# Alternating the transposes of a step with the score products in an attention kernel's TensorE queue

## The reference

```
h = layernorm(x) * (1 + ca) + sa
q = h @ wq + bq ; k, v = split(h @ wkv + bkv)          # 16 heads in 4 groups, head size 128
q, k = q + pe, k + pe                                  # a table of positions
probs = softmax(where(causal, q @ k.T / sqrt(128), -inf))
x = x + ga * ((probs @ v) @ wo)
h = layernorm(x) * (1 + cb) + sb
x = x + gb * moe(h)                                    # the best 2 of 8 experts, 256 -> 256
```

## Time and profile before

| | us |
|---|---|
| time, median of 3 runs | 930.61 (929.87 to 931.41) |
| span of the profiled execution | 929.5 |
| busy in it: TensorE products / weight loads | 904.2 / 782.2 |
| busy in it: VectorE / ScalarE / GpSimd | 782.4 / 535.9 / 274.5 |
| one steady frame | 22.4 |

### The profile page before, as it was taken

One profiled execution on the slowest core, in us unless ns is written; L12 is line 12 of the kernel. 1 busy time (PEld: TensorE's weight loads), 2 busy tenths in 40 slices (PEclk: granted clock), 3 DMA queues, 4 the chain that ended last, 5 costly groups with the idle time before them and its releaser, 6 DMA issues.

```text
span 929.5 us, 18019 instructions
## 1 busy us (share of the span) xinstructions
PE 904.2 (97%) x5353; PEld 782.2 (84%) x5353; DVE 782.4 (84%) x1775; ACT 535.9 (58%) x1224; POOL 274.5 (30%) x346
## 2 busy tenths in 40 slices
PE   5999999999999999999999999999999999999997
PEld 4788888888888888978888888888888889767775
DVE  6677888888888888888888888888888888899996
ACT  4587666666666666655666666666666655422231
POOL 4454222222222222133322222222222212466544
PEclk9999999999999999999999999999999999999999
DMA  6000000000000000100000000000000022100000
GB/s 215 7 12 13 12 13 12 11 17 17 11 11 11 11 11 7 57 6 1 24 12 12 14 12 11 11 11 11 11 11 11 12 86 81 46 12 18 23 17 24
DMA packets 23764, 21.60 MB, mean 23 GB/s; under 512 B 1530, under 2 KB 22564, under 8 KB 23716
## 3 DMA queue, kind: packets, MB, share of 16 engines
q1 hardware_dynamic: 23652, 20.99, 7.1%
q10 hardware_dynamic: 64, 0.02, 0.0%
HBM read 18.91 MB, written 2.10 MB: 23 GB/s over the span
## 4 chain that ended last, share of the span: by engine, by line
PE 87%; DVE 7%; issue 3%; ACT 2%; POOL 1%; DMA 1%; DVEq 0%; SPq 0%; POOLq 0%; ACTq 0%
PE ps_t L701 13%; PE ps_s L596 10%; PE ps_s L598 10%; PE ps_s L597 9%; PE ps_o L596 7%; PE ps_o L598 7%; PE ps_o L597 6%; PE ps_m L596 6%; PE ps_m L598 6%; PE ps_m L597 6%; PE ps_o L711 1%; PE ps_m L937 1%; PE ps_t L596 1%; PE ps_s L681 1%; DMA wmod_sb<-in_L_wmod_dram 1%
## 5 line engine op out<-in xcount | busy, mean ns | idle before, releaser
L992 ACT ACTIVATE pt_hi<-ps_t 128x512 fp32r<-128x512 f32 (+2 forms) x320 | 170.8, 534 | 143.3 <-PE ps_t L701 143.2
L1042 ACT ACTIVATE probs<-ps_s,neg_max 128x128 f32<-128x128 f32 (+7 forms) x256 | 189.8, 742 | 78.7 <-DVE neg_max L1336 74.4
L1345 DVE TENSOR_TENSOR pt_lo<-ps_t,pt_hi 128x512 fp32r<-128x512 f32 (+2 forms) x320 | 192.5, 602 | 12.6 <-ACT pt_hi L992 7.6
L1336 DVE TENSOR_REDUCE neg_max<-ps_s 128x1 f32<-128x128 f32 (+7 forms) x256 | 192.7, 753 | 3.7
L701 PE MATMUL ps_t<-ident,probs 128*128 128x128 f32 x1152 | 188.7, 272 | 2.1 <-DVE pt_lo L1345 2.1
L483 POOL TENSOR_TENSOR q_lo<-raw,q_hi 128x512 fp32r<-128x512 f32 x60 | 77.4, 1290 | 359.1 <-ACT q_hi L992 359.1
L701 PEld LDWEIGHTS ps_t<-ident,probs 128*128 128x128 f32 x1152 | 141.7, 140 | 27.1 <-DVE pt_lo L1345 8.9
L596 PE MATMUL ps_s<-k_hi,q_lo 128*128 128x512 f32 (+2 forms) x354 | 148.8, 420 | 2.3 <-ACT probs L1042 2.3
L1383 DVE SCALAR_TENSOR_TENSOR acc<-ps_m,rsum,acc 128x256 f32<-128x256 f32 x256 | 111.6, 478 | 24.3 <-PE ps_m L598 24.3
L1330 DVE TENSOR_TENSOR ps_s<-ps_s,mask 128x128 f32<-128x128 f32 x256 | 75.8, 296 | 56.9 <-PE ps_s L598 50.1
L598 PE MATMUL ps_s<-k_hi,q_hi 128*128 128x512 f32 (+2 forms) x354 | 123.5, 349 | 0.0
(11 more groups left out here) (180 smaller groups left out, 1718.0 us busy)
## 6 DMA issues: line engine op xcount, KB each, us to landing
wq_raw<-in_L_attn_wq_dram SPq DMA_DIRECT2D x32, 128.0 KB, 2.2
wo_raw<-in_L_attn_wo_dram SPq DMA_DIRECT2D x32, 128.0 KB, 2.0
wkv_raw<-in_L_attn_wkv_dram SPq DMA_DIRECT2D x2, 1024.0 KB, 6.5
we_raw<-in_L_ffn_expert_w_dram SPq DMA_DIRECT2D x1, 2048.0 KB, 10.1
x_again<-in_L_attn_x_dram SPq DMA_DIRECT2D x2, 1024.0 KB, 9.3
out_dram<-y_out SPq DMA_DIRECT2D x16, 128.0 KB, 1.7
acc<-in_L_attn_x_dram SPq DMA_DIRECT2D x2, 512.0 KB, 3.9
wmod_sb<-in_L_wmod_dram SPq DMA_DIRECT2D x2, 512.0 KB, 8.0
```

Source lines behind the costliest of these rows:

```text
L992: return nc.scalar.activation(dst, src, ACT.Copy, scale=scale)
L1042: nc.scalar.activation(probs[par][:, prob_offset(i):prob_offset(i) + w], ps_s[:, i % 2, col:col + w], ACT.Exp, bias=neg_max[:, par, i:i + ...
L1336: nc.vector.tensor_reduce(neg_max[:, par, i:i + 1], ps_s[:, i % 2, col:col + w], AXIS_X, ALU.max, negate=True).then_inc(max_set, 1)
L1345: nc.vector.tensor_tensor(pt_lo[:, q % PT, lo:CH], ps_t[:, q % 2, lo:CH], pt_hi[:, q % PT, lo:CH].bitcast(F32), ALU.subtract).then_inc(pt_ ...
```

## The change

In a frame that has a next head, all steps but 0 and 10 call a new function, `turn_and_score`, in the place of `turn_probs` and `score_piece`. It has the same waits and issues the same instructions, in another order: first transpose, first score product, second transpose, second product, third transpose, third product, then what is left of the transposes. The wait for the exponential stands in front of the first score product, and so ahead of all transposes but the first. The last transpose still releases ScalarE and the third product VectorE.

```diff
+            def turn_and_score(n, par, q, first, g):
...
+                tiles = list(range(max(j, c * TPC), (c + 1) * TPC))
+                turned = turn(tiles[0])
+                i, c0, w, ends = PIECES[q]
+                if i in (1, TPC) and q == FIRST_PIECE[i]:
+                    pe.wait_ge(q_lo_set, (n + 1) * NC + (i // TPC + 1))
+                if q == FIRST_PIECE[i]:
+                    pe.wait_ge(exp_set, (n + 1) * NT + (i - 1))
...
+                nc.tensor.matmul(out, q_lo[1 - par][:, rows], k_hi[:, g, keys], start=True, stop=False)
+                for t in tiles[1:2]:
+                    turned = turn(t)
+                nc.tensor.matmul(out, q_hi[1 - par][:, rows], k_lo[:, g, keys], start=False, stop=False)
+                for t in tiles[2:3]:
+                    turned = turn(t)
+                scored = nc.tensor.matmul(out, q_hi[1 - par][:, rows], k_hi[:, g, keys], start=False, stop=True)
+                if ends:
+                    scored.then_inc(s_mm, 1)
+                for t in tiles[3:]:
+                    turned = turn(t)
+                turned.then_inc(t_mm, 1)
...
                 for q in range(NS):
-                    turn_probs(n, par, q, first)
+                    mixed_step = nxt and q not in (0, 10)
+                    if mixed_step:
+                        turn_and_score(n, par, q, first, (l + 1) % G)
+                    else:
+                        turn_probs(n, par, q, first)
...
-                    if nxt:
+                    if nxt and not mixed_step:
                         score_piece(n + 1, 1 - par, (l + 1) % G, q, False)
```

More of the change, by code:

```diff
@@ L702, in turn_probs, with turn @@
                 last.then_inc(t_mm, 1)
+            def turn_and_score(n, par, q, first, g):
+                c, j = STEPS[q]
+                if j == 0:
+                    pe.wait_ge(exp_set, n * NT + (c + 1) * TPC)
+                if (q - 2) % NS in LAST_STEP and not (first and q < 2):
+                    pe.wait_ge(pt_hi_set, n * NS + (q - 1))
+                elif not (first and q < 2):
+                    pe.wait_ge(pt_lo_set, n * CUTS + cuts_before(max(q - 1, 0)))
+                def turn(i):
+                    p0 = prob_offset(i) + j * P
+                    col = (i - c * TPC) * P
+                    return pe.transpose(ps_t[:, q % 2, col:col + P], probs[par][:, p0:p0 + P], ident[:, :])
+                tiles = list(range(max(j, c * TPC), (c + 1) * TPC))
[5 more added lines that the diff above has]
+                    pe.wait_ge(exp_set, (n + 1) * NT + (i - 1))
+                rows = slice(i * P, (i + 1) * P)
+                col = score_offset(i) + c0
+                keys = slice(c0, c0 + w)
+                out = ps_s[:, i % 2, col:col + w]
+                nc.tensor.matmul(out, q_lo[1 - par][:, rows], k_hi[:, g, keys], start=True, stop=False)
[10 more added lines that the diff above has]
+                turned.then_inc(t_mm, 1)
             def weigh_values(n, g, q, first):
```

## The result

The changed kernel takes 946.09 us (median of 4 runs, 945.48 to 946.92) against 931.01 us for the kernel before on the same chip; the ratio is 1.0161, 95% interval 1.0147 to 1.0175. The forecast was 947.1. The span of the profiled execution is 943.7 us (929.5 before), and a steady frame takes 22.85 us (22.41; medians of 20 steady frames, from the first transpose's load of one frame to that of the next). 30 x 0.446 = 13.4 us are in the steady pace. The first frames of the two batch halves lost 0.84 and 0.90 us, together 0.9 more than two steady frames, and with these the 14.2 us between the two spans are accounted for within 0.1.

A forecast was written before the change was run, and what follows sets the result against it. TensorE's full queue bounds the kernel. Per frame 0.25 + 0.04 + 0.21 + 0.05 = 0.55 us, times 30 = 16.5 us; span 929.5 becomes 946.0, plus 1.1 gives 947.1 us; range 934 to 954.

The forecast's parts named there:

- The price of a transpose: In TensorE's queue a transpose costs 0.11 us, whether four stand in a row or one stands between products.
- Rival C: Faster: the next product's load hides under the product before; gain 33 us, 898 us; chance 0.05.
- Changeovers: 20 new pairs of switches between transposes and products per frame cost TensorE 0.13 us, bounds 0 and 0.20.
- Steps 2 and 3: Score product stalls 0.10 us for the first exponential; the next step's wait for VectorE swallows half, leaving about 0.05.
- Step 4: Score product waits 0.17 us for row tile 2's exponential, three transposes queued behind it; the step ends 0.25 us later.
- Step 6: Value product waits 0.21 us for the output's low part on VectorE; 0.50 us late, TensorE itself 0.29 late.
- Steps 7 to 9: Only switches cost, 0.05 us; VectorE and ScalarE run up to 1.2 us later but VectorE catches up within the frame.
- rival D: Lateness of ScalarE and VectorE carries into the next frame; about 0.9 us a frame, 957.6 us; chance 0.08.
- A: Only the switches between transposes and products cost: 3.9 us, 934.5 us; chance 0.08.
- B: The score product's wait costs, the value product's wait for the output's low part does not: 10.2 us, 940.8; chance 0.14.
- E: Nothing measurable, as TensorE's queue reaches every wait later than thought: 930.6 us; chance 0.05.
- The sign to look for: TensorE's wait list gains some 30 score-product and some 30 value-product entries, about 0.2 us each; frames 22.95 us.

The follow-up runs named there:

- the kernel with two transposes ahead: Changed kernel with step 5 in the old order and two transposes ahead of the score product at step 4: 936.13 us, ratio 1.0060.
- the new step 0: Kernel before, with step 0's first score product ahead of the six query products: 929.16 us, ratio 0.9983; timed again 929.41 us, 0.9981.
- the output first: Changed kernel, but at step 5 ScalarE and VectorE take the output's high and low parts before the transposed block's: 940.40 us, ratio 1.0104.

## Why the prediction was right, point by point

- **What bounds.** Right: what held the queue in a frame came back in the time at least thirty times over. The whole change and the three kernels with one wait or only steps 4 and 5 alternated gave 3.4 to 3.6 us for each 0.1 us; the kernel with two transposes ahead gave more, 5.4 us for 0.12.
- **The price of a transpose.** Right that the order doesn't change it: 0.11 us in a row and 0.11 alternated. Rival C (a faster kernel) is excluded by the frames of 22.44 and 22.32 us with six steps alternated, and by the spacing that it named: in the changed step 6, with a transpose between them, the loads of the 512-wide products are 0.34 and 0.35 us apart, where C wanted under 0.30.

```profile
298.66 0.19 PEld L730 LDWEIGHTS ps_s<-k_hi,q_lo 128*128 128x128 f32 x1
...
299.00 0.19 PEld L733 LDWEIGHTS ps_s<-k_lo,q_hi 128*128 128x128 f32 x1
...
299.35 0.19 PEld L736 LDWEIGHTS ps_s<-k_hi,q_hi 128*128 128x128 f32 x1
```

- **Changeovers.** The term that was mis-sized. I took 0.13 us a frame for 20 pairs; 14 pairs cost at most 0.03 us in the frame (22.44 against 22.41) and 0.1% (0.02 to 0.20%) in the time, and with the new step 0 nothing (22.32 with and without). The 0.01 us by which a transpose follows a 256-wide product late isn't lost at each changeover. This is most of the 0.10 us a frame by which the forecast was too high (3 us); the first frames of the two halves, which I took for ordinary ones, gave 0.9 back. So the span was forecast at 946.0 and is 943.7, 2.3 us less. That the time came within 1.0 us is in part luck: the 1.1 us that I took from span to time is 1.8 within one execution, and the median before moved up by 0.4 us with its fourth run.
- **Steps 2 and 3.** The stall at step 2 was 0.10 as forecast; step 3 swallowed all of it, not half. The first transpose of step 4 starts 7.07 us into the frame in both kernels (290.40 - 283.33, 295.35 - 288.28). The weight loads' list of waits shows the idle time that took it up, first before and then after. It also corrects my reading of TensorE's list, in which this wait seemed to be 2.1 us in the whole run:

```profile
PEld ps_t L701 <- DVE pt_lo L1345: 8.9, 33, 1.0
```

```profile
PEld ps_t L701 <- DVE pt_lo L1388: 2.3, 4, 1.0
```

- **Step 4.** The step ends 0.24 us late; forecast 0.25, as 0.05 carried over and a wait of 0.17. Measured: nothing carried over, and 0.23 waited.
- **Step 6.** The value product was forecast 0.50 late and is 0.46 late; the wait was forecast at 0.21 and is 0.20 in the frame shown. The chain is the forecast one link by link, and both ways of cutting it (the old order at step 5, the output first) remove the wait. My value of 0.29 us for TensorE's own arrival was 0.04 too high: with the output first, which keeps TensorE's order and has no wait here, the value product is 0.25 late.
- **Steps 7 to 9.** VectorE catches up as forecast. The first mask of step 11 waits for TensorE almost as long as before, so rival D is out:

```profile
311.02 0.30 DVE L1373 TENSOR_TENSOR ps_s<-ps_s,mask 128x128 f32<-128x128 f32 x1 [1.29 <-PE ps_s L736]
```

- **Rivals A, B and E.** A (changeovers alone) and E (nothing) fall with the run in which only steps 4 and 5 are alternated; B (one wait of the two) with the run in which step 4 is undone and 7.7 us stay.
- **The sign to look for.** I wanted some 30 entries of each kind in the list of waits. The list had 25 of the first (and 7 for the same line without a named releaser) and 3 of the second. Taken alone it would have spoken for rival B.

## What to carry to other kernels

When an engine's queue has next to no idle time, as here, a new order of the same instructions gains nothing unless it takes out a wait (22.32 us with and without alternation at the six steps), but it can lose: for each wait that is moved forward, take the distance moved less the slack in front of it, and for each signal that is moved back, follow its chain to the next wait of the full queue and do the same. Here margins of 0.08 and 0.10 us decided 15 us, because a frame repeats 30 times. Look for such margins before moving anything, and put work ahead of the wait, not behind it.

## What the hardware showed that I had not expected

Between fp32 transposes and reduced-fp32 products next to nothing is lost by switching at every instruction: 14 more changes there and back per frame cost 0.03 us in 22.4 in one pair of kernels and 0.00 in the other. And a stall of a product need not show in its engine's idle time. The value product of step 6, held up by 0.20 us, has no idle time in front of it in TensorE's records; it is recorded at 0.50 us instead of 0.40, and the product after it starts 0.34 us later instead of 0.23. First before, then with the change:

```profile
295.30 0.40 PE L596 MATMUL ps_o<-pt_hi,v_lo 128*128 128x512 f32 x1
295.53 0.40 PE L597 MATMUL ps_o<-pt_lo,v_hi 128*128 128x512 f32 x1
```

```profile
300.61 0.50 PE L596 MATMUL ps_o<-pt_hi,v_lo 128*128 128x512 f32 x1
...
300.95 0.40 PE L597 MATMUL ps_o<-pt_lo,v_hi 128*128 128x512 f32 x1
```

A longer record is no proof of a stall, though: a 512-wide product right behind a transpose is recorded at 0.48 us without any wait (298.68 in the changed kernel).
